# An adaLN block on one core: all but two of the piece sums on VectorE, own buffers for four tiles of residual rows, and a new order of the first stage

## The reference

```python
mod = (silu(c) @ wmod).reshape(1, 6, 1, 1024)      # c: 1 x 1024, wmod: 1024 x 6144
sa, ca, ga, sb, cb, gb = (mod[:, i] for i in range(6))
ga = sign(ga) * max(abs(ga), 0.25)                  # gb alike
h = layernorm(x) * (1 + ca) + sa                    # x: 2048 x 1024
x = x + ga * (h @ (weight * block_mask).T + bias)   # mask in blocks of 32 x 32
h = layernorm(x) * (1 + cb) + sb
x = x + gb * ffn(h)     # silu(h @ gate.T) * (h @ up.T) @ down.T, int weights with scales, width 2752
```

## Time and profile before

| what | value |
|---|---|
| median of 3 runs | 1203.4 us (1202.77 to 1205.47) |
| the profiled execution | 1204.89 us, span of its trace 1202.9 us |
| mean granted TensorE clock | 0.97 of full |
| PE busy in 0 to 300 us | 236.6 us of 300 |
| PE busy in 300 to 1203 us | 894 us of 903 |
| DVE busy in 90 to 150 us / in 150 to 180 us | 49.1 of 60 / 15.0 of 30 |

### The profile page before, as it was taken

The page is one execution under the profiler, slowest core; times in us unless marked ns, Lnnn a source line. Parts: engine busy times, 40 slices in busy tenths (PEclk is TensorE's granted clock), DMA queues, the critical chain, the costliest instruction groups (busy, mean ns, idle before and its releaser), DMA issues.

```text
span 1202.9 us, 13039 instructions
## 1 busy us (share of the span) xinstructions
PE 1130.6 (94%) x4770; PEld 534.7 (44%) x4770; DVE 658.2 (55%) x834; ACT 407.5 (34%) x734; POOL 353.3 (29%) x357
## 2 busy tenths in 40 slices
PE   5798667998999999999999999999999999999998
PEld 2544343454544444444444444444444444444444
DVE  4677846898567586666666666655442222222222
ACT  0316114454554444454545444443331000000000
POOL 1014714634565434334433453332110000000000
PEclk9798967998999999999999999999999999999999
DMA  9992113253534334555556555531446334344320
GB/s 348 402 316 70 36 35 105 70 175 93 157 125 160 88 96 119 141 149 139 147 143 153 136 147 141 141 80 44 179 140 228 134 123 151 105 143 153 111 100 35
DMA packets 89663, 167.08 MB, mean 139 GB/s; under 512 B 18496, under 2 KB 53056, under 8 KB 86912
## 3 DMA queue, kind: packets, MB, share of 16 engines
q1 hardware_dynamic: 72288, 125.33, 33.1%
q0 software_dynamic: 11504, 40.38, 11.4%
q10 hardware_dynamic: 5808, 0.55, 0.4%
HBM read 117.47 MB, written 48.76 MB: 138 GB/s over the span
## 4 chain that ended last, share of the span: by engine, by line
PE 78%; DVE 11%; POOL 3%; issue 3%; ACT 2%; DMA 2%; DVEq 1%; SPq 1%; ACTq 0%; POOLq 0%
PE pA L1052 28%; PE pB L1052 13%; PE pA L1148 12%; PE pB L1148 11%; PE pA L944 9%; DVE work L1258 3%; DMA work<-in_L_wmod 2%; DVE work L1191 1%; PE pB L933 1%; ACT work L730 1%; DVE work L1200 1%; POOL work L570 1%; DVEq L1167 1%; DVE small L1166 1%; DVE work L1179 1%
## 5 line engine op out<-in xcount | busy, mean ns | idle before, releaser
L1052 PE MATMUL pA<-work 128*128 128x512 f16 x1680 | 378.5, 380 | 5.7 <-ACT work L845 2.9
L1052 PEld LDWEIGHTS pA<-work 128*128 128x128 f16 x1680 | 164.5, 98 | 205.5 <-ACT work L845 3.9
L944 PE MATMUL pA<-work 128*128 128x512 f32 x512 | 235.6, 617 | 9.4 <-ACT work L730 8.0
L1052 PE MATMUL pB<-work 128*128 128x512 f16 x752 | 176.2, 379 | 0.0
L944 PEld LDWEIGHTS pA<-work 128*128 128x128 f32 x512 | 99.8, 199 | 129.7 <-issue 118.1
L1148 PE MATMUL pA<-work 128*128 128x512 f16 x672 | 147.7, 379 | 0.0
L668 POOL DMA_DIRECT2D h_scratch<-work x84 | 64.4, 767 | 283.3 <-DVE work L1404 277.2
L845 ACT ACTIVATE work<-pA 128x512 f32<-128x512 f32 x126 | 75.2, 597 | 208.2 <-PE pA L1052 208.0
L1148 PE MATMUL pB<-work 128*128 128x512 f16 x630 | 138.4, 379 | 0.0
L1404 DVE SCALAR_TENSOR_TENSOR work<-work 128x512 f16<-128x512 f16 x84 | 67.5, 803 | 115.7 <-ACT work L851 115.6
L730 ACT ACTIVATE work<-pB,small 128x128 f32<-128x128 f32 x256 | 92.6, 486 | 91.0 <-DVE small L1335 38.2
(11 more groups left out here) (124 smaller groups left out, 990.9 us busy)
## 6 DMA issues: line engine op xcount, KB each, us to landing
work<-in_L_wmod SPq DMA_DIRECT2D x12, 2048.0 KB, 17.9
work<-h_scratch SPq DMA_DIRECT2D x16, 1376.0 KB, 6.1
h_scratch<-work POOLq DMA_DIRECT2D x84, 256.0 KB, 3.2
work<-in_L_ffn_gate_w SPq DMA_DIRECT2D x84, 128.0 KB, 3.6
work<-in_L_ffn_up_w SPq DMA_DIRECT2D x84, 128.0 KB, 3.6
work<-in_L_ffn_down_w SPq DMA_DIRECT2D x96, 112.0 KB, 2.5
work<-in_L_attn_data SPq DMA_DIRECT2D x16, 512.0 KB, 4.5
x_scratch<-work POOLq DMA_DIRECT2D x16, 512.0 KB, 5.7
```

The costliest lines, as they stand in the source:

```text
L944: last = pe.matmul(pA[:, 2 * par(t) + h, :], hT1[par(t)][:, c, :], wT[:, c, h * H:(h + 1) * H], start=(c == 0), stop=(c == KT - 1))
L1052: last = pe.matmul(ps, w[:, m, c], bc[b][:, mv_, s, c], start=begin, stop=(i == n - 1 and c == KT // 2 - 1 and s == 1), skip_group_check=True)
```

## The change

- The pieces 7 and 9 are summed by `sum_half` on DVE as the others are; `scale_right` and `sum_right` go. In `sum_half` the eight multiply-adds of v = 3 and 4 run at full width in place in the piece, and only the last writes the accumulator in two halves (before: all eight in two halves of 256).
- The tiles 2 to 5 get x1 buffers of their own (`x1_late`), so that their residuals wait for no z2 and no store. Means and roots of both norms have six places.
- The tiles 2 and 3 get their own `hf` and `tb`, so that `second_input(2)` and `(3)` do not wait for the splits of pair 0, 1.
- Order: the pieces 4 and 5 (for ga) are loaded and summed ahead of the lower half of mask and weight, and `gate_row(2)` stands ahead of the transposes of the weight's lower rows. The residuals up to tile 5 stand ahead of the factors of the second half, and the second norm's transposes are placed by the tables `MID` and `END`: 0 at t = 3, then 1 and 2 at t = 6, 3 and 4 at t = 7, 5 at t = 8, 6 and 7 at t = 9, from t = 10 t - 2 as before. The second columns, the reduce and `scales` now stand between the residuals of the tiles 4 and 5.
- The bias load and the ten small loads are started by SP, behind a wait for the last transpose of the weight. The bias shares its buffer with a weight row block.

```diff
@@ SP
+                if g == 0:
+                    load_piece(4)
+                    load_piece(5)
             for i in range(2):
                 sp.wait_ge(x_copied, i + 1)
                 sp.wait_ge(z_done[0], i + 1)
                 load_x(i + 2)
-            load_piece(4)
-            load_piece(5)
-            for m in range(6, 10):
-                load_piece(m)
+            load_piece(6)
+            load_piece(7)
+            sp.wait_ge(w_turned, 2 * KT)
+            sp.dma_start(gab, bias.rearrange("(o n) -> o n", o=1).to_broadcast([P, D])).then_inc(bias_loaded, 16)
+            load_piece(8)
+            load_piece(9)
+            for s_in, s_col, r in ((gate_s, sgs, 0), (up_s, sus, P // 2)):
...
@@ POOL
-            rstd_of(0, 3)
 
             for t in range(NT + 1):
+                if t == 5:
+                    pool.wait_ge(bounds_in, 4)
+                    pool.partition_all_reduce(bma, bmx, P, bass.bass_isa.ReduceOp.max).then_inc(bounds_out, 1)
                 if 3 <= t <= LAST - 2:
                     rstd_of(0, t + 2)
...
-                if t == 3:
-                    sum_right(3)
-                    sum_right(4)
-                if t == 4:
-                    pool.wait_ge(bounds_in, 4)
-                    pool.partition_all_reduce(bma, bmx, P, bass.bass_isa.ReduceOp.max).then_inc(bounds_out, 1)
...
@@ ACT
-                if t == 2:
-                    scale_right(3)
-                    scale_right(4)
-                if t == 4:
+                if t == 5:
                     act.wait_ge(cols2_ready, 2)
-                    wait_summed(act, 9)
                     second_input(0)
...
@@ PE
             attend(0, 0)
+            attend(1, 0, range(0, 4))
             mask_total_of(1)
-            attend(1, 0, range(0, 4))
-            turn_rows(4)
             attend(1, 0, range(4, KT))
-            for n in range(5, KT):
+            pe.wait_ge(mask_bits, 2)
+            pe.wait_ge(cols1_ready, 2)
+            gate_row(2, rowp[0])
+            for n in range(4, KT):
                 turn_rows(n)
...
-            gate_row(2, rowp[0])
@@ DVE
             mask_rows_of(0)
+            for h in range(2):
+                sum_half(2, h)
             mask_rows_of(1)
             norm1(2)
-            for h in range(2):
-                sum_half(2, h)
...
-            norm1(3)
             gate_a()
+            sum_half(3, 0)
             residual_of_evacuated(0)
             normalise(1, 0)
+            norm1(3)
             residual_of_evacuated(1)
             norm1(4)
             dve.wait_ge(scales_loaded, 16 * 2 * (A + 1))
             bound_of(2, sgs)
             bound_of(3, sus)
+            sum_half(3, 1)
             residual(2)
             norm1(5)
-            sum_half(3, 0)
             normalise(1, 1)
             sum_half(4, 0)
             residual(3)
-            stats1(6)
+            sum_half(4, 1)
+            norm1(6)
+            residual(4)
             cols2()
-            normalise(0, 6)
+            norm1(7)
             scales()
-            for t in range(4, NT + 1):
...
+            residual(5)
+            sum_half(5, 0)
+            for t in range(6, NT + 1):
+                if t <= LAST - 2:
                     norm1(t + 2)
+                if t in (6, 7, 8):
+                    lo_part(2 * t - 12)
...
+                if t in MID and t > 3 and t <= LAST:
+                    normalise(1, MID[t] + 1)
                 if t <= LAST:
                     residual(t)
...
+                if t in END:
+                    normalise(1, END[t] + 1)
+                if t in (6, 7, 8):
+                    lo_part(2 * t - 11)
+                if t == 9:
                     sum_half(5, 1)
```

More of the change, by code:

```diff
@@ L35, in adaln_kernel @@
     W_MAX = 128.0
-    SMALL = 208
+    SMALL = 224
     LAST = NT - 1
@@ L178, in adaln_kernel @@
         acc = [acc_a, gbs, acc_a, hf[0], acc_a, gbs]
+        x1_late = [late[:, D * k:D * (k + 1)] for k in range(4)]
+        o = O_BC0 + 3 * 2 * HE
+        hf_late = [at(o + 4 * D * k, 4 * D) for k in range(2)]
+        tb_late = at(o + 2 * 4 * D, 4 * D)
+        assert 3 * 4 * D <= 2 * HE
         used = [0]
@@ L194, in adaln_kernel @@
         bnst = [cols(12) for _ in range(2)]
-        mv = [[cols(2)] * 2, [cols(2), cols(2)]]
+        mv = [[cols(2)] * 6, [cols(2) for _ in range(6)]]
         ve = [cols(1) for _ in range(2)]
-        rstd = [[cols(1)] * 2, [cols(1), cols(1)]]
+        rstd = [[cols(1)] * 6, [cols(1) for _ in range(6)]]
         mhalf = cols(1)
@@ L356, in adaln_kernel @@
         TAIL_UNIT = [k[0] for k in UNITS].index("tail")
+        MID = {3: 0, 6: 1, 7: 3, 8: 5, 9: 6, **{t: t - 2 for t in range(10, NT + 1)}}
+        END = {6: 2, 7: 4, 9: 7}
+        SUMS_AT = {6: 1, 7: 3, 8: 5, 10: 7, **{t: t - 2 for t in range(11, LAST + 1, 2)}}
         NCONST = 13
@@ L362, in par, with place, x1_of, hf_of @@
             return t % 2
-        def halves_of(v, h, src):
-            if v in (0, 1, 2, 5):
-                return [(acc[v][:, h * H:(h + 1) * H], src)]
-            by_tile = acc[v].rearrange("p (c a i) -> p a c i", c=KT, a=A)
-            return [(by_tile[:, 2 * h + k], src[:, k * KA:(k + 1) * KA].rearrange("p (c i) -> p c i", c=KT))
-                    for k in range(A // 2)]
+        def place(t):
+            return t if t < 6 else t % 2
+        def x1_of(t):
+            return x1_late[t - 2] if 2 <= t < 6 else x1[t % 2]
+        def hf_of(r):
+            return hf_late if r in (2, 3) else hf
+        def tb_of(r):
+            return tb_late if r in (2, 3) else tb
         def wait_summed(eng, m):
-            if m in DVE_SUMMED:
-                eng.wait_ge(dve_summed, DVE_SUMMED[m])
-            else:
-                eng.wait_ge(pool_summed, POOL_SUMMED[m])
+            n = SUMMED.index(m) + 1
+            eng.wait_ge(dve_summed, n + sum(1 for k in SUMMED[:n] if 6 <= k < 10))
         def mask_rows(eng, r):
@@ L448, in _ @@
                 load_x(i + 2)
-            load_piece(4)
-            load_piece(5)
-            for m in range(6, 10):
-                load_piece(m)
+            load_piece(6)
[5 more added lines that the diff above has]
+            for s_in, s_col, r in ((gate_s, sgs, 0), (up_s, sus, P // 2)):
+                for a in range(A):
+                    src = s_in[FA * a:FA * (a + 1), :].rearrange("(c i) o -> i (c o)", i=Q)
+                    sp.dma_start(s_col[Q * a:Q * (a + 1), 0:FT], src).then_inc(scales_loaded, 16)
+                sp.dma_start(s_col[r:r + FL, FT:NF], s_in[FT * P:F, :]).then_inc(scales_loaded, 16)
             for t in range(1, NT + 1):
@@ L646, in _ @@
                         pool.tensor_tensor(xg[i], xg[i], gab, ALU.add).then_inc(xg_ready, 1)
-                if t in (5, 6):
-                    sums(2 * t - 9)
-                elif t >= 7 and t % 2 == 1:
-                    sums(t - 2)
+                if t in SUMS_AT:
+                    sums(SUMS_AT[t])
                 if t <= LAST:
@@ L710, in _ @@
             act.activation(csil, cvec, ACT.Silu).then_inc(silu_c_done, 1)
-            def scale_right(v):
-                m = 2 * v + 1
-                act.wait_ge(piece_loaded[m], 16)
-                w = mp[m].rearrange("p (t n) -> p t n", t=KT)
-                for t in range(KT):
-                    last = act.activation(w[:, t], w[:, t], ACT.Copy, scale=csil[:, t:t + 1])
-                last.then_inc(piece_scaled, 1)
             for v in range(2):
@@ L819, in _ @@
             for t in range(2, NT + 1):
-                if 7 <= t <= LAST and t != 13:
+                if 11 <= t <= LAST and t != 13:
                     hi_part(t - 3)
```

187 lines of the change are left out of this document (88 added, 99 removed).

## The result

| what | before | after |
|---|---|---|
| median (range) | 1204.43 us (1202.77 to 1206.72, 4 runs) | 1193.85 us (1192.35 to 1196.22, 4 runs) |
| the profiled execution, its span | 1204.89, 1202.9 us | 1192.35, 1190.4 us |
| PE busy in 100 to 150 us / 150 to 180 us | 40.8 / 18.5 us | 46.8 / 24.4 us |
| PE busy in 180 to 210 us, with the granted clock | 22.2 us, 0.78 | 20.5 us, 0.75 |

The account below looks back on a forecast made before the run. PE waits and low clock, caused by DVE and POOL's chain, bound the stretch: 53.7 us falls to 35.6, 18.1 less, plus 2.4 from an earlier start, 20.5 in all, giving 1182.9 us; range 1173 to 1192.

Parts of the forecast that it names:

- What bounds the kernel, and where: PE waits and low clock before 300 us, 53.7 us in the stretch, all from one DVE and POOL chain.
- The start: Masking to ga: ga and its bias ready at 81.7 instead of 94.2; first attend of tile 2 at 90.9.
- DVE's chain up to the columns: Tile 3's norm done at 103.4, piece 9's sum at 148.9; the 15.43 us wait shrinks to 2.7.
- Blocking between DVE and POOL: Piece sums on DVE: each POOL addition falling beside one is charged its full 2.3 us.
- The rival that collisions cost less: DVE and POOL collide less than charged, up to the wait for tile 2's z2: 1171 to 1177 us; chance 0.20.
- The reduce, and what stands behind it: POOL, then DVE: reduce 6.95 us to 166.8, root and normalise of tile 7 1.6, scales 3.7, factors at 172.1.
- my first rival: POOL's switch back behind the reduce costs 6.5 us again, delaying tile 7's root and the factors: 1189.4 us; chance 0.20.
- What followed from it: After the factors at 172.1, tile 2's z2 comes at 192.5 and PE waits 8.9 us for it, plus 3.1 clock.
- From tile 7 on: PE waits only 1.7 us at tile 11's first attend and 4.9 at tile 9's transpose; tile 11's second attend at 275.
- The other rivals: SP's load queue becomes the bound, 1209 us at a 50 us hold, chance 0.05; no change in time, 0.04.
- the wait in the middle: No-change rival: the middle PE wait returns whole through a DVE chain 20 us longer, giving the old time; chance 0.04.

Follow-up runs that it names:

- the experiment: Changed kernel with the inverse root of tile 7 ahead of the reduce on POOL instead of behind it: 1187.86 us, ratio to the kernel before 0.9848.
- the run with the reduce ahead of the addition: Changed kernel, piece 11 loaded later, reduce and tile 7's root ahead of a bias addition and store on POOL, scales before tile 7's normalise: 1184.64 us, ratio 0.9825.
- the kernel with both edits: Changed kernel with tile 7's root ahead of the reduce and piece 11 loaded one step later: 1182.22 us, ratio to the kernel before 0.9804.
- the extra reduce: Changed kernel plus a second reduce, result unread, early on POOL behind its first masking: 1194.72 us in a single timing.

## Why the prediction was wrong, point by point

| term (us) | forecast | measured |
|---|---|---|
| first attend of tile 2 starts | 90.9 | 89.9 |
| wait ahead of tile 3's transpose, and clock | 5.6 + 3.1 | 4.11 + 2.8 |
| wait for the columns, and clock | 2.7 + 2.5 | 2.24 + 4.5 |
| wait ahead of tile 7's transpose | none | 3.23 |
| wait ahead of the second lower transpose, and clock | none | 5.49 + 2.7 |
| wait for tile 2's z2, and clock | 8.9 + 3.1 | 6.33 + 2.8 |
| waits at t = 10 and 11 | 1.7 | 0.66 + 1.25 |
| wait ahead of tile 9's transpose, and clock | 4.9 + 3.1 | 5.56 + 2.1 |
| sum of the waits | 35.6 | 43.8 |

The clock terms are the rows behind a wait against the same rows at the high clock (1.97 against 1.04, 8.77 against 6.95, and so on). The two starts give the lost time a second way: 284.86 - 89.9 = 195.0, with 1.2 of low clock in the row itself 196.2, less 151.6 of work: 44.6, so 0.8 us lie in waits too short for the table. That is 9.0 more than forecast, and the start is 1.0 better: 8.0 us of gain are missing, and 20.5 - 8.0 = 12.5 us is what the spans show (1202.9 - 1190.4). The medians miss about 2 us more, which is where the two profiled executions happen to lie.

- **What bounds the kernel, and where:** right. All of the gain lies ahead of 300 us, and every wait in the table is one on the chain of DVE and POOL.
- **The start:** right. ga's clamp began at 74.48 (my sum: 75.6), and ga and its bias were ready at 79.6 instead of 81.7; the bias had landed by 78.4. The small loads on SP delayed nothing. That the stretch begins 1.0 us earlier than forecast is no merit of the sum: in other executions it begins up to 4 us later.
- **DVE's chain up to the columns:** right, a little too long. Tile 3's norm was done at 100.9 (forecast 103.4), piece 9's sum at 145.4 (148.9). The 15.43 us of the earlier trace rows became 2.24, though the low clock behind it cost 4.5 and not 2.5 us: I had bounded the cost by that of the columns alone, 3.3, and left out the attend behind them, which took 9.70 here (and 8.91 before) instead of 6.95.
- **Blocking between DVE and POOL:** right. The same six multiply-adds took 4.69 us alone and 6.65 beside one of POOL's additions (timeline of DVE):

```profile
127.89 4.69 DVE L1266 SCALAR_TENSOR_TENSOR work<-work,small 128x512 f32<-128x512 f32 x6
...
137.90 6.65 DVE L1266 SCALAR_TENSOR_TENSOR work<-work,small 128x512 f32<-128x512 f32 x6
```

  I had charged 2.3 for an addition, and it is 1.96. The rival that collisions cost less falls. The sum with its last row in halves is 0.48 + 4.69 + 0.88, with gaps 6.0 us, for which I had taken 6.2. The Trainium skill ("SBUF — State Buffer", section Who interferes with whom) calls the pair of ports that the two engines share an exclusive lock, by which the later instruction waits out the earlier one. The trace agrees in the main: the sums lose 1.96 us beside an addition that lasts 2.61 us, so three quarters of it and not all.
- **The reduce, and what stands behind it:** this step failed, in two terms. First, "Root and normalise of tile 7, 1.6; scales, 3.7": the root takes that long, but POOL has to go back to its usual routines first, 7.29 us. This is my first rival, to which I gave 0.20; its price of 6.5 us was about right: 6.0 by the medians of the experiment, 7.8 by the ratios. I argued against it from the row at 185.35, which was no longer than others of its kind. That was a wrong reading: the cost stands as idle time ahead of the row, not in it, and the 13.96 us there had room for it. The Trainium skill ("GPSIMD Engine Reference", section Instruction dispatch) gives about 6 us for the first call of a freshly loaded routine; the run with the reduce ahead of the addition shows 5.70 for the way in, and the way back, 6.8 to 7.3, is not less. Second, "The reduce took 6.95 us from the last bound": I took the price of before over, with a store ahead of it but no large load. Even that was read too short: the switch instruction had already been started 0.8 us ahead of the last bound, so the way in was 7.33 us there (view by source line of the kernel before):

```profile
L641 POOLq MODIFY_POOL_CONFIG  x2: 1/1/1, 163.6 to 163.7; - x2
```

  The change starts piece 11's 2 MB at that instant, two steps earlier than before, and the way in became 10.68 us. The reduce nevertheless ended at 167.5 (forecast 166.8), since the chain ahead of it was 3 us faster than my sum: these two errors hid each other by luck, and what shows in the time is the way back.
- **What followed from it:** the factors were ready at 180.1 instead of 172.1. DVE's work from there to tile 2's z2 took the 20 us that I had given it, so z2 came 7.4 us late, and that is nearly all of the 8.0 that are missing; the rest is the sum of smaller errors both ways. PE stood first for tile 7 (its root waited with the factors), then for the lower rows' second transpose, then for z2 of tile 2, which came at 199.9 instead of 192.5. With both causes taken away the factors came at 170.0, z2 at 189.8, and the time was 1182.22 us against my 1182.9.
- **From tile 7 on:** right. 0.66, 1.25 and 5.56 us where I had 1.7 and 4.9. The second attend of tile 11 started at 284.86; the sum gives 298.65 - 20.5 = 278.2 (the 275 in the prediction is 3 us short of its own sum), and 284.86 - 278.2 = 6.7 us, with the 1.2 us of low clock in the row itself 7.9, is again the missing part. In the kernel with both edits it started at 274.83.
- **The other rivals:** SP was never the bound, and the wait in the middle did not come back.
- **A part I had not weighed:** I named the second split set as a condition in half a sentence, and gave it no price. By experiment all of the gain is lost without it. What the x1 buffers and the new order of the start are worth by themselves stays open.
- **Range and chances:** the rival stood in the range with its own 1189.4, but its sum kept every other term. A second, independent 3 us in the same place (piece 11's load) wasn't in the bounds, although the order on SP that the change writes down puts a 2 MB load there.

## What to carry to other kernels

An idle stretch that nobody waits in may hide a cost: before an instruction is moved up to stand behind a special operation, bound the gap by all of it, and don't argue the cost away because the next row has its usual length. Put short work on which others wait ahead of a switch of POOL's routines, and let the switch instruction come early, where its price runs beside a wait (the extra reduce showed this; moving the real reduce earlier gained no time here, since an instruction behind the way back then held DVE). When buffers and order are changed together, ask for each buffer what the new order would do without it: here the one that looked least important was what the gain hung on.

## What the runs showed of the chip

- A switch of POOL's routines counts from its own instruction and runs beside a wait (48.1 to 55.1 us, with the awaited copy ending at 55.01). It is paid each time, and on the way back too: 6.83 to 7.29 us in the nine kernels where nothing else held the next row.
- The way in took 5.6 to 5.7 us where next to nothing was moved meanwhile (1 GB/s, three kernels). It took 6.7 to 7.6 where a store by POOL and a load of x by SP, 512 KB each, had been started less than 2 us earlier (135 to 144 GB/s, four kernels, before among them), so which of the two matters isn't told. It took 9.6 to 10.7 where the 2 MB load was started up to 1 us ahead of the switch as well (295 to 332 GB/s, after and four variants). In these five the reduce ran within 2 us of the end of the full traffic (about 400 GB/s), where the other four came 3 to 4 us behind it. Only the step from 10.7 to 7.6 was tested by an edit; why it is so is open, since beside steady full traffic (406 GB/s, the early reduce) it was at most 7.1.
